# Two schedules of one eight-core kernel: how it loads ahead, broadcasts rows and ends its last stage

## The reference, cut to what matters

```
xn = layernorm(x)                                   # x: 4 x 4096 x 2048
Bu = xn @ (gamma * B).T                             # complex, 256 states
h_t = A * h_(t-1) + Bu_t                            # scan over 4096 tokens
s  = Re(C h) + D * xn
v  = (rmsnorm(xn) * w1) @ wv + bv ;  h = xn + v @ wo
h2 = rmsnorm(h) * w2
mlp = (silu(h2 @ w_gate) * (h2 @ w_up)) @ w_down    # 2048 -> 5632 -> 2048
g = silu(where(sigmoid(xn . w_router + b) > 0.5, h + mlp, xn))
out = x + s * g
```

## Time and profile before

| what | us |
|---|---|
| median of 3 runs | 4316.14 |
| lowest and highest run | 3928.8, 4331.77 |
| the profiled execution | 3928.8 |
| its span (slowest core, number 7) | 3927.0 |
| spans of the eight cores | 3878.2 to 3927.0 |
| TensorE busy, share of the span | 2692.0, 69% |
| VectorE busy | 1038.9, 26% |

### The profile page before, as it was taken

How to read it: one execution, slowest core, us unless ns; L and a number is a source line. 1 busy time by engine, 2 the same in 40 slices (tenths; PEclk the granted TensorE clock), 3 DMA queues, 4 the chain that set the end, 5 groups by cost and what they waited for, 6 DMA issues and landing times.

```text
span 3927.0 us, 31011 instructions; the slowest of 8 cores (3878.2 to 3927.0 us)
## 1 busy us (share of the span) xinstructions
PE 2692.0 (69%) x11744; PEld 1148.1 (29%) x11744; DVE 1038.9 (26%) x1201; ACT 414.5 (11%) x491; POOL 362.8 (9%) x311
## 2 busy tenths in 40 slices
PE   6130524488369999966666637882999999566666
PEld 1010211133124444422222212331444444222222
DVE  1557375713411000111122231133001100212222
ACT  2130000210210000000000012102000000000000
POOL 0000000011011111100000001110111111000000
PEclk9675768699689999988888868996999999788887
DMA  6050524579777777765566655895777777566664
GB/s 184 9 182 24 170 69 145 101 82 157 132 95 77 75 75 76 75 84 80 101 108 109 109 116 65 99 163 139 75 76 75 76 76 75 91 106 108 109 108 78
DMA packets 732340, 388.27 MB, mean 99 GB/s; under 512 B 683018, under 2 KB 685082, under 8 KB 727453
## 3 DMA queue, kind: packets, MB, share of 16 engines
q0 software_dynamic: 679728, 178.28, 46.3%
q1 hardware_dynamic: 52466, 208.01, 17.7%
HBM read 514.12 MB, written 50.38 MB: 144 GB/s over the span
## 4 chain that ended last, share of the span: by engine, by line
PE 51%; DMA 24%; DVE 13%; issue 4%; ACT 2%; PEld 2%; POOL 1%; DVEq 1%; PEldq 1%; SPq 0%; ACTq 0%; POOLq 0%
PE ps L155 51%; DMA arena<-down_p 10%; DMA arena<-xT 7%; DVE arena L159 7%; ACT arena L176 2%; DMA arena<-wv_p 2%; DMA arena<-xNB 2%; DVE arena L179 2%; PEld ps L155 2%; POOL arena L149 1%; DMA arena<-up_p 1%; DVE arena L163 1%; DMA hspill<-arena 1%; DVE arena L171 1%; DVEq L123 1%
## 5 line engine op out<-in xcount | busy, mean ns | idle before, releaser
L155 PE MATMUL ps<-arena 128*128 128x512 bf16 x11264 | 2555.6, 390 | 878.4 <-DMA arena<-down_p 424.1
L155 PEld LDWEIGHTS ps<-arena 128*128 128x128 bf16 x11264 | 1116.2, 100 | 2318.5 <-issue 1083.6
L159 DVE TENSOR_TENSOR arena<-arena,ps 128x512 bf16<-128x512 f32 (+1 forms) x240 | 165.1, 688 | 1177.4 <-ACT arena L176 1129.2
L159 DVE TENSOR_TENSOR arena<-arena 128x1024 f32<-128x1024 f32 (+8 forms) x195 | 216.5, 1110 | 897.8 <-ACT arena L176 851.6
L176 ACT ACTIVATE arena<-ps 128x512 f32<-128x512 f32 x240 | 143.5, 598 | 2061.5 <-PE ps L155 2039.2
L176 ACT ACTIVATE arena<-arena 128x2048 bf16<-128x2048 bf16 (+4 forms) x103 | 140.5, 1364 | 708.6 <-DVE arena L159 309.9
L149 POOL DMA_DIRECT2D arena<-gate_p x88 | 100.6, 1143 | 1172.3 <-PE ps L155 998.5
L155 PE MATMUL ps<-arena,ones_bf 128*1 128x512 bf16 x256 | 73.2, 407 | 184.2 <-DVE arena L179 119.5
L159 DVE TENSOR_TENSOR arena<-arena,m_bc 128x1024 f32<-128x1024 f32 x64 | 78.4, 1225 | 422.5 <-DMA arena<-xT 379.4
L149 POOL DMA_DIRECT2D arena<-down_p x64 | 85.9, 1347 | 988.0 <-PE ps L155 988.0
L179 DVE CAST arena<-arena 128x1024 bf16<-128x1024 f32 (+1 forms) x96 | 83.7, 872 | 220.4 <-PE ps L155 92.5
(11 more groups left out here) (49 smaller groups left out, 379.9 us busy)
## 6 DMA issues: line engine op xcount, KB each, us to landing
arena<-xT SPq DMA_DIRECT2D x128, 512.0 KB, 5.8
arena<-gate_p POOLq DMA_DIRECT2D x88, 512.0 KB, 7.5
arena<-up_p POOLq DMA_DIRECT2D x88, 512.0 KB, 9.3
arena<-down_p POOLq DMA_DIRECT2D x64, 704.0 KB, 10.3
arena<-xT SPq DMA_DIRECT2D x16, 1024.0 KB, 6.7
arena<-xNB SPq DMA_DIRECT2D x16, 1024.0 KB, 10.7
arena<-xNB SPq DMA_DIRECT2D x32, 512.0 KB, 5.9
arena<-wv_p POOLq DMA_DIRECT2D x32, 512.0 KB, 6.6
```

The costliest lines, as they stand in the source:

```text
L155: E.matmul(o, l, r, start=a, stop=b), inc=inc)
L159: E.tensor_tensor(o, a, b, al), inc=inc)
```

## The change

The diff in six parts (line numbers in the diff are those of the file before).

1. Order of the preamble: the powers of A are written first, then the own statistics, the own rows with their broadcasts, and only then the neighbour's statistics and rows.
2. `stats_pass`, `bu_pass` and phase 3 use two load slots in place of four and three; `bu_pass` issues its first loads behind waits for all VectorE work so far.
3. `bcast` no longer goes through HBM: a one-row float32 matmul with `ones1` spreads 512 columns into PSUM (banks 6 and 7 in turn), and VectorE copies them out, four times for a row of 2048.
4. Phase 4: `hsq4` has two copies, and the sums of squares lag by two planes; `ts2` becomes two `tsc`; the wait on the spills (`sO`) stands before the row arithmetic.
5. Phase 6, weights: `mk_half` is marked at the 22nd and at the 44th matmul of each group, and TensorE waits for `dring[1]` only before the second 22.
6. Phase 6, epilogue: it runs per group of 512 columns, reads the down sums from PSUM on VectorE without ScalarE's copy, and h, x and xn are loaded as six pieces of 256 KB per plane.

```diff
@@ stats_pass (moved behind the powers of A)
+    xb = [arF(64 + 8 * i, T) for i in range(2)]
-            wait("sync", sV, ring_v.get(sl))
-            wait("sync", sT, ring_t.get(sl))
+            if k >= 2:
+                wait("sync", sV, mkv[k - 2])
+                wait("sync", sT, mkt[k - 2])
@@ bcast
-        mk1 = dma("sync", sBr, scr, row_ap[:, 0:n])
-        wait("sync", sBr, mk1)
-        return dma("sync", sBr, dst[:, 0:n], scr.partition_broadcast(128))
+        for q in range(qn):
+            bank = 6 + (q % 2)
+            wait("tensor", sV, ps_rd.get(bank, 0))
+            mk1 = mm(ps[bank][:, :], ones1[:, :], row_ap[:, q * 512:(q + 1) * 512],
+                     True, True, inc=sT)
+            wait("vector", sT, mk1)
+            mk_ev = cp("vector", dst[:, q * 512:(q + 1) * 512], ps[bank][:, :],
+                       inc=sV)
@@ bu_pass
+        wait("sync", sG, sG.v)
+        wait("sync", sV, sV.v)
+            if qp == 1:
+                wait("sync", sV, sV.v)
-                sl = k % 3
-                wait("sync", sV, ring_v.get(sl))
+                sl = k % 2
+                if k >= 2:
+                    wait("sync", sV, mkg_cast[k - 2])
@@ phase4
+        wait("vector", sO, sO.v)
         cp("vector", rms2_bc[0:1, 0:512], ps[4][0:1, :])
         cp("vector", rms2_bc[0:1, 512:1024], ps[5][0:1, :])
-        ts2("vector", rms2_bc[0:1, :], rms2_bc[0:1, :], INV_D, 1e-6,
-            AL.mult, AL.add)
+        tsc("vector", rms2_bc[0:1, :], rms2_bc[0:1, :], INV_D, AL.mult)
+        tsc("vector", rms2_bc[0:1, :], rms2_bc[0:1, :], 1e-6, AL.add)
@@ phase6
                 if q == 0:
                     wait("tensor", sDn[0], mk_w0)
-                    wait("tensor", sDn[1], mk_w1)
                 for j in range(22):
-                    mm(ps[bankd][:, :], dring[0][:, j * 128:(j + 1) * 128],
-                       ff_pl[j][:, q * 512:(q + 1) * 512], j == 0, False)
+                    mk_half[(d, q, 0)] = mm(
+                        ps[bankd][:, :], dring[0][:, j * 128:(j + 1) * 128],
+                        ff_pl[j][:, q * 512:(q + 1) * 512], j == 0, False,
+                        inc=sT if j == 21 else None)
+                if q == 0:
+                    wait("tensor", sDn[1], mk_w1)
-                mk_half[(d, q, 0)] = mk_half[(d, q, 1)] = sT.v
-                mk_evd[idx] = act(t6b[:, q * 512:(q + 1) * 512], ps[bankd][:, :],
-                                  AF.Identity, inc=sS)
+                tt("vector", tb, p6h[q], ps[bankd][:, :], AL.add)
```

More of the change, by code:

```diff
@@ L419, in build_nc @@
     mk_rr = milestone("vector")
-    wait("sync", sV, mk_rr)
+    wait("tensor", sV, mk_rr)
     bcast(rowm, rr1_bc)
[L422 to L428, removed]
     onescol = arF(140, 1)
@@ L446, in build_nc @@
     tsc("vector", row_tmp[0:1, :], row_tmp[0:1, :], br_sb[0:1, 0:1], AL.add)
-    tsc("vector", row_S1[0:1, :].bitcast(mybir.dt.uint8)[0:1, 0:T],
-        row_tmp[0:1, :], 0.0, AL.is_gt)
+    tsc("vector", row_tmp[0:1, :], row_tmp[0:1, :], 0.0, AL.is_gt)
     mk_msk = milestone("vector")
-    wait("sync", sV, mk_msk)
-    bcast(row_S1[0:1, :].bitcast(mybir.dt.uint8), mask_bc, u8=True)
-    wait("vector", sBr, sBr.v)
+    wait("tensor", sV, mk_msk)
+    bcast(row_tmp[0:1, :], mask_bc)
+    pmark("P0stats_nb")
+    fence(("tensor",))
+    mk_ns = stats_pass(xNB.ap(), False)
+    wait("vector", sT, mk_ns)
+    for q in range(4):
+        cp("vector", row2[0:1, q * 512:(q + 1) * 512], ps[q][0:1, :])
+    for q in range(4):
+        cp("vector", row_sx2[0:1, q * 512:(q + 1) * 512], ps[4 + q][0:1, :])
     tsc("vector", rowm, rowm, INV_D, AL.mult)
@@ L491, in build_nc @@
     upl = [arF(8 * i, T) for i in range(4)]
+    xbh = [arF(112 + 4 * i, TS) for i in range(2)]
     xbf_s = [arB(136 + 2 * i, TS) for i in range(2)]
@@ L740, in phase4 @@
         mk_row = milestone("vector")
-        wait("sync", sV, mk_row)
-        mk_r2bc = bcast(rms2_bc[0:1, :], rms2_bc, qn=2)
-        wait("vector", sBr, mk_r2bc)
+        wait("tensor", sV, mk_row)
+        for q in range(2):
+            bank = 6 + q
+            wait("tensor", sV, ps_rd.get(bank, 0))
+            mk1 = mm(ps[bank][:, :], ones1[:, :],
+                     rms2_bc[0:1, q * 512:(q + 1) * 512], True, True, inc=sT)
+            wait("vector", sT, mk1)
+            ps_rd[bank] = cp("vector", rms2_bc[:, q * 512:(q + 1) * 512],
+                             ps[bank][:, :], inc=sV)
         mk_psfree4 = milestone("vector")
-        h2tmp = [xb4, x4tmp]
-        wait("vector", sO, sO.v)
+        h2tmp = [xb4, arF(136, TS)]
         mk_h2 = {}
@@ L883, in phase6 @@
                     wait("tensor", sBc, mk_C)
-                wait("tensor", sV, mk_ep.get(d - 2))
                 for pi in range(4):
```

233 lines of the change are left out of this document (129 added, 104 removed).

## The result

The changed kernel takes 0.963 of the time before (95% interval 0.9602 to 0.9658): some 145 us less, not the 315 forecast. Median of 12 runs 3910.68 us (3765.33 to 4044.21), beside a median of 4063.98 (3906.29 to 4331.77) of the kernel before. The profiled execution took 3779.89 us, against 3928.8. The views of the earlier trace rows for the kernel after: the slowest core, the chain by line, the stretches of phase 5 and of both phases 6 (length, PE, PEld, DVE, ACT, POOL, clock, DMA share, GB/s), and who waited for whom.

The account below looks back on a forecast made before the run. Phase 6, 28% of the span, was taken as bound by no engine, with TensorE waiting for `down_p` once per plane. The sum: 3928.8 - 334 (weights) - 10 (epilogue) - 5 (phase 4) + 34 (preamble) = 3614 us, range 3550 to 4000.

Parts of the forecast that it names:

- A gap of 2.3 us is shorter than the one after which the clock fell, so I take all 96 matmuls at 216 ns.: Phase 6: after the short idle gap the clock stays up, so a plane's 96 matmuls take 20.8 us.
- 2 x 8.8 - 10.3 = 7.3: Phase 6: a first weight half loaded alone lands 7.3 us after issue, leaving TensorE idle 2.3 us.
- 0.7, near the lower end: Phase 6: SP's store and loads beside the weights cost 0.7 us per plane, between bounds of nothing and 3.8.
- The contention rival: Phase 6: SP's loads stretch each weight load by the full 3.8 us, +93, giving 3707 us; chance 0.20.
- The epilogue costs nothing there.: Phase 6: the epilogue per 1024 columns, 9.8 us, hides under 23.8 us of matmuls and costs nothing inside the phase.
- The preamble, +34: Preamble: new order, two slots, broadcasts and Bu passes together cost +34 us, bounds about -25 and +170.
- My 80 us: Preamble: a statistics pass with two slots takes 80 us; for the neighbour's pass, 58 before, that is +21.
- Bu passes: Preamble: two slots make a plane 2.6 us, not 2.3, +19 us, and each pass's first load adds +5.
- Phase 3 "nothing", phase 4 "-5": Phase 3's two slots cost nothing; phase 4's new broadcast saves 5 us for both tiles, bounds 0 and -12.
- The tails: End of each phase 6: only one half of the epilogue is left, -4.8 us each, -10 together.
- Early release brings nothing: Rival, phase 6: both weight halves still land together, so the phase stays as it was, 3948 us; chance 0.05.
- TensorE stays at the low level: Rival, phase 6: matmuls cost 433 ns, a plane 41.6 us, giving 4188 us, slower than before; chance 0.03.

Follow-up runs that it names:

- The filler: Changed kernel with 16 matmuls on old data added behind each plane of phase 6, in the gap: ratio 0.9507, lowest 3724.21 us.
- the release alone: Kernel before with only part 5, the first half of the down weights released at the 22nd matmul of q = 1: ratio 0.9368, lowest 3652.73 us.

## Why the prediction was wrong in size

The direction and the cause were right; the sum missed by 166 us: 113 in the two phases 6, 34 ahead of the first, 19 between them.

- *"A gap of 2.3 us is shorter than the one after which the clock fell, so I take all 96 matmuls at 216 ns."* This step failed first. The gap was 4.7 and the clock fell in it, in the changed kernel's rows above as early as 1926 to 1928. Matmuls were busy for 369.8 and 362.5 us, not 332.8: 67 us over both phases, the largest part of the miss. The filler shows it by taking the fall away (-41 us). The inference was weak from the start, since it rested on one gap. In the same trace of the kernel before, TensorE stopped at 3397.24, and the clock had begun to fall before 3400, less than 3 us later (columns as above):

```profile
3398.00:3400.00 2.00, 0.00 (x0) 0.00 (x0) 1.78 (x2) 0.00 (x0) 1.60 (x2) 0.83 0.35 31
```

  Nor would a gap of the forecast's own 2.3 to 3.0 us have been safe. In the kernel without loads and stores (core 1), two gaps of 2.8 us came out differently: 96 matmuls in 22.57 us behind the first, in 4.91 + 16.13 = 21.04 behind the second (between the two parts it waited 0.90 us for the second half):

```profile
1881.96 22.57 PE L153 MATMUL ps<-arena 128*128 128x512 bf16 x96 [2.77 <-DMA arena<-down_p]
1907.31 4.91 PE L153 MATMUL ps<-arena 128*128 128x512 bf16 x22 [2.79 <-DMA arena<-down_p]
1913.12 16.13 PE L153 MATMUL ps<-arena 128*128 128x512 bf16 x74 [0.90 <-DMA arena<-down_p]
```

- *The first half's landing, "2 x 8.8 - 10.3 = 7.3".* That step inferred the first of a pair from a median of two, with SP silent. Measured before: 7.8. In the new place, 9.2. The gaps came to 66.8 and 71.2 us, not 45: 48 us.
- *Contention, "0.7, near the lower end, since only the last microsecond meets them".* Mis-sized. The rival's "SP is silent while the first half is on its way" was wrong too: the epilogue of q = 0 ends 0.4 us behind the half's issue and stores. But leaving that store out still gave 9.0 us. The contention rival (3707) had the direction and a price of 3.8 where 1.5 was measured; its mechanism, SP's transfers beside the weights, is shown for the pair of loads (17.5 against 12.2 us) and not for the first half here. Its total is nearer to what was measured than my forecast, in part by luck, since it too left out the clock.
- *"The epilogue costs nothing there."* Wrong by 25 us a phase beside the old one (3691 against 3653). VectorE's work is hidden, as said; what its transfers cost is not, whether by their number or otherwise. Without the release the same epilogue makes the two phases 155 us longer than before (624 and 615 against 544.5 and 540.2).
- *The preamble, +34.* To phase 3 it was +62 (medians over the cores, 678.8 to 740.6). Own pass and powers: -17.5 on the slowest cores, not -30. The neighbour's pass: 83 us (first cast at 305.3 to the row copies at 388.7) where 58 had been, +25 and not +21. My 80 us were nearly right: the changed `stats_pass` holds a slot until the squares' matmul is done, in the neighbour's pass too, where the kernel before let it go at the cast. SP waited for TensorE in it 14 times, and not once in the kernel before with two slots, where the pass lost only about 10 us. Rows with their broadcasts (all that lies between the passes): +18, not +14. Bu passes: +42, not +29; 38 of it came back with a third slot. A plane took 2.7 to 2.9 us from cast to cast, where I chose 2.6, and 2.1 to 2.3 before, where I read 2.3.
- *Phase 3 "nothing", phase 4 "-5".* Phase 3 +3.5 and phase 4 +6.4 in the first tile, again medians. The row section was right, the planes' loop was left out of the sum.
- *The tails.* -3.7 at the end of the program, near the -4.8 forecast.
- *Early release brings nothing* is refuted by the release alone. *TensorE stays at the low level* did not happen (clock 0.90 and 0.92 in the phases), but its mechanism in small, 2 to 2.5 us a plane, is what the first point describes.

## What to carry to other kernels

When a wait on a load is shortened, compare what is left of the gap with the clock as the trace shows it: a gap that remains costs twice, as time and as clock. Finer pieces took another 121 us off the release alone (3653 to 3532), and idle work in the gap 41 us off the changed kernel. Before making an engine off the path faster, look at what it issues when it ends: here a slow epilogue kept SP's transfers out of the weights' way, and the faster one made the two phases 155 us longer; holding the loads back returned 115 us of the whole time (4144 to 4028). Parts of a change should be priced apart: one of these six carried the whole gain (3653), and that one with smaller pieces and more load slots reached 3516.

## What the runs showed of the hardware that was not expected

The granted clock is lost within a gap of 4.3 us, in the 2 us from 1926 to 1928, and returns only at 1934, 5 us into dense work; the kernel before held it at 1.00 for more than 4 us of idleness in the earlier trace rows. So one gap can come out either way, and two gaps of 2.8 us in one kernel did. A pair of 704 KB weight loads needed 12.2 us of TensorE's waiting with SP's loads held back and 17.5 with these issued 6 us behind it. And 1 MB loads gained nothing from four in flight over two (landing 6.7 against 4.9 us between 30 and 100 us in the own pass), while the Bu passes with their 512 KB loads gained with every slot up to four (302, 267 and 251 us). A first weight half landed in 9.5 us with nothing of the core's own SP queue beside it, and in 7.7 when all cores left their loads and stores out.
